# A decoder layer on one core: order of the prologue and of the first body changed on five queues

## What is computed

```python
x = x + self_attention(layernorm(x))          # 16 heads of 16, rotary positions, causal window of 64
x = x + cross_attention(layernorm(x), ctx)    # 16 heads of 8 over 256 channels, mask rows and columns
x = x + experts(layernorm(x))                 # 8 experts, top 2 by sigmoid score + bias, and a shared one
```

## Time and profile before

| | us |
|---|---|
| median of 3 runs (lowest, highest) | 422.46 (421.8, 425.17) |
| the profiled execution, own time | 422.43 |
| its span, first to last instruction | 420.6 |
| PE busy / DVE busy / ACT busy / POOL busy | 330.3 / 271.1 / 140.1 / 103.7 |
| mean granted clock of TensorE | 0.886 |

### The profile page before, as it was taken

One profiled execution on the slowest core, in us unless ns is written; L12 is line 12 of the kernel. 1 busy time (PEld: TensorE's weight loads), 2 busy tenths in 40 slices (PEclk: granted clock), 3 DMA queues, 4 the chain that ended last, 5 costly groups with the idle time before them and its releaser, 6 DMA issues.

```text
span 420.6 us, 6660 instructions
## 1 busy us (share of the span) xinstructions
PE 330.3 (79%) x2532; PEld 207.6 (49%) x2550; DVE 271.1 (64%) x500; ACT 140.1 (33%) x221; POOL 103.7 (25%) x125
## 2 busy tenths in 40 slices
PE   2685875694667979779979789998774979979787
PEld 2563443451322436458733336884222646636676
DVE  4557895299634387966872788778477445543755
...
DMA packets 31115, 28.27 MB, mean 67 GB/s; under 512 B 5964, under 2 KB 28204, under 8 KB 31084
## 3 DMA queue, kind: packets, MB, share of 16 engines
...
## 4 chain that ended last, share of the span: by engine, by line
PE 49%; DVE 22%; issue 10%; ACT 6%; SPq 5%; DMA 4%; POOL 3%; DVEq 0%; POOLq 0%; ACTq 0%
PE ps L941 13%; PE ps L975 6%; PE ps L863 5%; DVE max L1777 5%; PE ps L620 4%; ACT prob L1264 4%; PE ps L841 3%; PE ps L798 3%; SPq L440 2%; PE ps L631 2%; DVE max L1716 2%; DVE o1s L1731 2%; PE ps L884 1%; PE ps L659 1%; DVE u L1830 1%
## 5 line engine op out<-in xcount | busy, mean ns | idle before, releaser
L1777 DVE TENSOR_REDUCE max<-ps 128x4 f32<-128x1024 f32 x64 | 77.0, 1220 | 39.1 <-PE ps L798 39.1
L1264 ACT ACTIVATE prob<-ps 128x1024 f32<-128x1024 f32 x64 | 63.9, 1026 | 58.9 <-PE ps L841 58.7
L941 PE MATMUL ps<-xn1T,w_sb 128*128 128x256 f32 (+1 forms) x360 | 76.0, 360 | 6.1 <-DVE u L1830 5.6
L941 PEld LDWEIGHTS ps<-xn1T,w_sb 128*128 128x128 f32 x360 | 61.4, 201 | 17.1 <-DVE u L1830 7.5
L1508 POOL TENSOR_TENSOR u_times_u<-u 128x256 f32<-128x256 f32 (+1 forms) x45 | 29.1, 647 | 106.3 <-DVE u L1830 65.4
L863 PE MATMUL ps<-prob,v 128*32 128x256 f32 x512 | 41.9, 417 | 7.0 <-ACT prob L1264 6.7
L975 PE MATMUL ps<-w_sb,hT 128*128 128x256 f32 x144 | 40.5, 401 | 5.2 <-DVE hT L1839 5.2
L1716 DVE TENSOR_REDUCE max<-ps 128x4 f32<-128x512 f32 x32 | 21.3, 686 | 23.3 <-PE ps L659 23.2
L1244 ACT ACTIVATE prob<-ps 128x512 f32<-128x512 f32 x32 | 19.1, 598 | 45.6 <-PE ps L687 45.6
L1300 ACT ACTIVATE tanh_u<-u 128x256 f32<-128x256 f32 (+1 forms) x45 | 16.7, 372 | 49.7 <-DVE u L1830 45.2
L1830 DVE TENSOR_TENSOR u<-ps,g_bc 128x512 f32<-128x512 f32 (+1 forms) x40 | 23.2, 580 | 14.2 <-PE ps L941 9.6
...
## 6 DMA issues: line engine op xcount, KB each, us to landing
...
```

What stands on the lines that cost most here:

```text
L941: mm = pe.matmul(ps[:, banks_of(i, batches).up[n % 2], D * w + cols.start:D * w + cols.stop], w13_sb[:, e, k, w, :], xn3T[:, k, cols], sta ...
L1264: act.activation(prob[:, 2 * (u % 4):2 * (u % 4) + 2, :], ps[:, bank:bank + 2, :], ACT.Exp).then_inc(exp2, 1)
L1777: v.tensor_reduce(max2[:, a].rearrange("p t (j u) -> p j t u", j=2)[:, :, :, u], ps[:, bank:bank + 2, :].rearrange("p j (t s) -> p j t s", ...
```

## The change

In the prologue ScalarE copies pair 1's tokens between its casts of pair 0's query and key; TensorE does the key and value projections of cross pair 0 ahead of the turn of the maxima; the three memsets of the mask rows go to the start of VectorE's program and the five copies to ScalarE, behind `self_out(0, 1)`, with semaphores `mrow_fills` and `mrow_copies`. On SyncE the key's parts of pair 0 go before the store of the mask rows, `load_x(2)` goes before the mask rows' loads, the experts' first six weights are loaded in one piece behind the query's parts of pair 0, the key's parts of pair 1 go right behind `scores_b1` 16 and ahead of the maxima of batch 0, and the maxima of batch 1 go behind the first part of the query of pair 1. In body 0 `out` goes behind `exp 0` and `max 3`, `query` behind `max 5` and `exp 3`, `turn` ahead of `exp 6`, with residual, norm, bias and casts one or two groups later. The wait for the experts' weights counts four DMAs instead of six.

```diff
--- before.py
+++ after.py
@@ -104,11 +104,11 @@
 SPREAD = ((SEL, 1), (DOWN, 2))
 LAST_PAIR = (1, 1, 1, 2, 1, 2, 1, 2)
 FIRST_STEPS = ((), (), (0, 1), (2,), (3,), (4,), (5,), (6,), (7,))
-FIRST_JOBS = (("max", 0, 1, ("max", 8)), ("max", 1, 2, None), ("max", 2, 1, ("max", 9)), ("out", 0, 0, None),
-              ("exp", 0, 0, None), ("max", 3, 2, ("max", 10)), ("exp", 1, 1, ("max", 11)), ("max", 4, 2, ("max", 12)),
-              ("exp", 2, 0, ("exp", 1)), ("query", 0, 0, None), ("max", 5, 2, ("max", 13)), ("exp", 3, 1, ("exp", 2)),
+FIRST_JOBS = (("max", 0, 1, ("max", 8)), ("max", 1, 2, None), ("max", 2, 1, ("max", 9)), ("exp", 0, 0, None),
+              ("max", 3, 2, ("max", 10)), ("out", 0, 0, None), ("exp", 1, 1, ("max", 11)), ("max", 4, 2, ("max", 12)),
+              ("exp", 2, 0, ("exp", 1)), ("max", 5, 2, ("max", 13)), ("exp", 3, 1, ("exp", 2)), ("query", 0, 0, None),
               ("max", 6, 2, ("max", 14)), ("exp", 4, 0, ("exp", 3)), ("max", 7, 2, ("max", 15)),
-              ("exp", 5, 1, ("exp", 4)), ("exp", 6, 0, ("exp", 5)), ("turn", 0, 0, None), ("exp", 7, 1, ("exp", 6)))
+              ("exp", 5, 1, ("exp", 4)), ("turn", 0, 0, None), ("exp", 6, 0, ("exp", 5)), ("exp", 7, 1, ("exp", 6)))
 FIRST_BANKS = (2, 3, 0, 7)
 LEAD = ((0, 1), (2,), (3,), (), (4,), (5,), (6,), (), (7,))
 
@@ -296,7 +296,9 @@
         first_mid = [sem(f"first_{n}_mid") for n in "qk"]
         first_low = [sem(f"first_{n}_low") for n in "qk"]
         consts = sem("consts")
+        mrow_fills = sem("mrow_fills")
         mrow_chain = sem("mrow_chain")
+        mrow_copies = sem("mrow_copies")
         mrow_st = sem("mrow_st")
 
         var_ready = [sem(f"var_ready{n}") for n in range(3)]
@@ -491,7 +493,7 @@
                                  rows.broadcast_to([P, 2, cols.stop - cols.start])).then_inc(g_ld[q], 16)
 
             def mask_rows_store():
-                sp.wait_ge(mrow_chain, 11)
+                sp.wait_ge(mrow_copies, 5)
                 for n, rows in enumerate((mrow_q, mrow_k)):
                     for j in range(2):
                         sp.dma_start(d_mrow[n, :, :, j].rearrange("b s d t -> b s (d t)"),
@@ -552,32 +554,32 @@
             sp.wait_ge(v2_proj, 1)
             load_ctx(1)
             load_masks(1)
-            mask_rows_store()
             for c in range(3):
                 cross_part(0, 1, c)
-            load_experts(0, 3)
+            mask_rows_store()
+            sp.wait_ge(x1_ready, 1)
+            load_x(2)
             sp.wait_ge(mrow_st, 16 * 4)
             cross_mask_rows(0)
-            sp.wait_ge(x1_ready, 1)
-            load_x(2)
             for c in range(3):
                 cross_part(0, 0, c)
-            load_experts(3, 6)
+            load_experts(0, 6)
+            sp.wait_ge(scores_b1, 16)
+            for c in range(3):
+                cross_part(1, 1, c)
             cross_max(0, 0)
             for c in range(3):
                 self_part(2, c)
-            sp.wait_ge(scores_b1, 16)
             cross_mask_rows(1)
-            for c in range(3):
-                cross_part(1, 1, c)
             load_ctx(2)
             load_masks(2)
             sp.wait_ge(x1_ready, 2)
             load_x(3)
-            for c in range(3):
+            cross_part(1, 0, 0)
+            cross_max(0, 1)
+            for c in (1, 2):
                 cross_part(1, 0, c)
             load_experts(6, 9)
-            cross_max(0, 1)
             self_max(2)
             for i in range(1, PAIRS - 2):
                 body(i, True, True, True)
@@ -921,7 +923,7 @@
                 if n > 1:
                     pe.wait_ge(u_ready, u - 1)
                 if u == 0:
-                    pe.wait_ge(ld_experts, 16 * 6)
+                    pe.wait_ge(ld_experts, 16 * 4)
                 if n == 0:
                     pe.wait_ge(ez_ready, i + 1)
                     wait(pe, u_ready, 9 * i)
@@ -1075,9 +1077,9 @@
             pe.wait_ge(consts, 2)
             for c in range(8):
                 self_max_scores(0, c)
-            self_turn_max(0)
             cross_project_keys(0)
             cross_project_values(0)
+            self_turn_max(0)
             for step in range(9):
                 if step < 8:
                     self_exp_scores(0, step, (MISC, 0))
@@ -1373,9 +1375,9 @@
             act.dma_start(bqk_sb[:, 0:1], bq).then_inc(ld_cross, 16)
             act.dma_start(bqk_sb[:, 1:2], bk).then_inc(ld_cross, 16)
             act.dma_start(bv_sb[:], bv.broadcast_to([P, P])).then_inc(ld_cross, 16)
-            for n in range(2):
-                first_high_part(n)
+            first_high_part(0)
             self_tokens(1)
+            first_high_part(1)
             for n in range(2):
                 first_mid_part(n)
             act.wait_ge(first_high[1], 1)
@@ -1399,6 +1401,12 @@
                 if c == 4:
                     self_out(0, 0)
             self_out(0, 1)
+            act.wait_ge(mrow_chain, 10)
+            for r in (2, 3):
+                act.copy(mrow_q[:, 3 * r:3 * r + 3, :], mrow_q[:, 3:6, :]).then_inc(mrow_copies, 1)
+            for c in range(3):
+                src = mrow_q[:, c:c + 1, :]
+                act.copy(mrow_k[:, 3 + 3 * c:6 + 3 * c, :], src.broadcast_to([B, 3, D])).then_inc(mrow_copies, 1)
             cross_high(0, 0)
             cross_mid(0, 0)
             self_turn_max(1)
@@ -1421,9 +1429,9 @@
             for kind, u, pair, free in FIRST_JOBS:
                 if kind == "exp":
                     exponential(0, 0, u, pair)
-                    if u == 2:
+                    if u == 4:
                         cross_high(1, 0)
-                    if u == 4:
+                    if u == 6:
                         cross_mid(1, 0)
                 elif kind == "turn":
                     turn_max(0, 1)
@@ -1646,15 +1654,13 @@
                 ins.then_inc(ready, 1)
                 chain.end()
 
-            mrow = Chain(dve, mrow_chain, 11)
+            mrow = Chain(dve, mrow_chain, 10)
 
             def mask_rows():
 
                 mrow.start(0)
+                dve.wait_ge(mrow_fills, 1)
                 dve.wait_ge(mall_ld, 16)
-                v.memset(mrow_q[:, MASK_ROWS:2 * HD2, :], 0.0)
-                v.memset(mrow_k[:, MASK_ROWS:2 * HD2, :], 1.0)
-                v.memset(mrow_k[:, 0:3, :], 1.0)
                 mrow.link(v.tensor_scalar(m_pen[:], m_all[:], -1.0, 1.0, ALU.mult, ALU.add))
                 mrow.link(v.tensor_scalar(m_pen[:], m_pen[:], -NEG, None, ALU.mult))
                 for n, src in enumerate((m_pen, m_all)):
@@ -1666,14 +1672,7 @@
                         mrow.link(v.tensor_tensor(part[2], m_r[:, n, :], part[1], ALU.subtract))
                 v.tensor_tensor(mrow_q[:, 5, :], m_r[:, 1, :], mrow_q[:, 4, :], ALU.subtract).then_inc(mrow_chain, 1)
                 mrow.n += 1
-                dve.wait_ge(mrow_chain, mrow.n)
-                for r in (2, 3):
-                    v.tensor_copy(mrow_q[:, 3 * r:3 * r + 3, :], mrow_q[:, 3:6, :])
-                for c in range(3):
-                    src = mrow_q[:, c:c + 1, :]
-                    ins = v.tensor_copy(mrow_k[:, 3 + 3 * c:6 + 3 * c, :], src.broadcast_to([B, 3, D]))
                 assert mrow.n == 10
-                ins.then_inc(mrow_chain, 1)
 
             mp1 = Chain(dve, mp1_chain, 3)
             mp2 = Chain(dve, mp2_chain, 3)
@@ -1936,6 +1935,9 @@
                 cross_max_parts(i, 1)
                 second_batch(i, has_self, has_next)
 
+            v.memset(mrow_q[:, MASK_ROWS:2 * HD2, :], 0.0)
+            v.memset(mrow_k[:, MASK_ROWS:2 * HD2, :], 1.0)
+            v.memset(mrow_k[:, 0:3, :], 1.0).then_inc(mrow_fills, 1)
             dve.wait_ge(small_fills, 1)
             self_norm(0)
             dve.wait_ge(ld_ident, 16)
@@ -1988,10 +1990,10 @@
             for kind, u, pair, free in FIRST_JOBS:
                 if kind == "max":
                     cross_max(0, 1, u, pair)
-                    if u == 2:
+                    if u == 3:
                         self_residual(1)
                         cross_norm(1)
-                    if u == 4:
+                    if u == 5:
                         cross_query_bias(1)
             cross_max_parts(0, 1)
             second_batch(0, True, True)
```

## The result

The changed kernel took 407.84 us (median of 4 runs, 403.36 to 412.66), the kernel before 423.81 us in the same comparison (4 runs, 421.8 to 430.58): a ratio of 0.964, 95% interval 0.954 to 0.975. Executions of one kernel come in two states, and the ratio is taken from the fast ones, the medians from all. The forecast was 415.0, with 411.8 to 418.8 as its range. The direction was right; the gain was about twice the one forecast.

A forecast was written before the change was run, and what follows sets the result against it. The prediction took no single engine as the bound but chains of dependent steps and their waits, chiefly for pair 2's normalised tokens and `stack_1k<-parts`. Sum: 0 + 0 - 2.3 - 5.1 = -7.4, 422.43 to 415.0 us, range 411.8 to 418.8.

The forecast's parts named there:

- Prologue and mask rows: Start through the mask-row work: about 0 for the prologue, bounds -1.5 and +3, and 0 on the path for mask rows.
- early tokens: Prologue: token copy between the casts starts projections earlier; of 4 us on TensorE only 0.5 is left at the scores.
- both new gaps: Prologue: TensorE idle about 24 to 28 and 39 to 43 us, opened by the change.
- Load of x: Before 75.89 us: VectorE's 3.27 us wait for pair 2's x goes, token turn earlier; -2.3, bounds -2.4 and -1.2.
- second rival: Clock: slow work follows both new gaps, pair 0's exponent steps all take 1.5 us; +3, total 418.0; 12%.
- The stage behind it: After pair 2's token turn, up to 97.6 us: on-chip work only shifts along, no further gain.
- First body: ScalarE's 7.19 us wait for the key's transfers goes; batch 1 starts 7.4 earlier, 5.1 new, unknown ends -3 and -6.5.
- third rival: First body: shorter gap before max scores 5 keeps the clock up for query and values; another -1.5, 413.5; 15%.
- From the scores of batch 1 on: Everything behind batch 1's start, about 126 us: depends on these starts alone, shifts as a whole, no further gain.
- first rival: First body's stall is only replaced: body gives 2.5 instead of 5.1, x load 1.8, total 418.1; 15%.
- slow copies: Fourth rival, mask rows: ScalarE copies at 4.0 us each delay the load of x; +5, total 427.4; 4%.
- shift eaten later: Fifth rival: a later wait (key's transfers or pair 2's masks) eats the shift, no gain, 422; 9%.

The follow-up runs named there:

- b_lock: The kernel before, with GpSimd's low part of pair 1 waiting until the parts of the first maxima are written; ratio 0.994 of the kernel before (0.988 to 0.9997).
- u_keys: The changed kernel with the context's key and value projections behind the first turn of the maxima again; median 410.68 us (4 runs).
- u_x: The changed kernel with the load of x for pair 2 behind the mask rows' loads again; ten runs between 416.7 and 422.6 us.
- a_again: The changed kernel run once more, nothing edited; no total is stated, its batch 1 stage took 20.5 us against 22.0 in the first profile.
- a_lock: The changed kernel with GpSimd's low part of pair 1 waiting for the parts of the first maxima; median 409.25 us.
- u_row: The changed kernel with the row of batch 1's maxima behind all the query's parts and the load of experts again; 421.78 us, 0.9985 of the kernel before.
- u_jobs: The changed kernel with the old jobs table put back (order of output projection, query, turn, residual, norm, bias, casts); median 409.11 us.

## Why the forecast was off

**Prologue and mask rows, 0: right.** The 0.5 us of the early tokens did not appear at 28.82, the mask rows were hidden as said. The 0 holds for the sum of the stage and not for its parts: both new gaps are followed by slow work. The -2.0 in the profile is the draw against GpSimd: b_lock, the kernel before with none held, has 37.6 and 30.9, the kernel after 37.5 and 29.9. With the -0.5 of the next column it lies outside the bounds of -1.5 to +3 and has another reason than they named. Copies on ScalarE: forecast 0.8 each, measured 0.77.

**Load of x, -2.3: right, -2.6.** The row of pair 1's maxima was put at 3.7 us from issue to landing "as the row issued at 39.93 did"; that row was used at 44.03, 4.1 behind, which changes 74.1 to 74.5 and nothing in the sum. The second rival, slow work behind the two new gaps, came true in part: 0.63 us for the first scores at 28.82 (0.39 before) and for the exponent steps until 45.1, but not for all of them. It did not show as a loss of the two stages against the kernel before, which had its own slow steps until 48.4, and by ending later than the new ones they hid the cost of the second gap; u_keys, without the second gap, is about 2 us shorter there.

**The stage behind it, 0: wrong, -1.7 to -2.6.** "Everything up to 97.6 is on-chip and shifts along" took work for fixed that is done at either clock. The wait that was taken away had also kept the clock down: 0.50 until 82 us before, 1.00 from 72.8 in the changed kernel. With the wait put back (u_x) the stage is 25.9; without it 23.9, and 23.0 in a_again and a_lock.

**First body, -5.1: right, -5.8.** The steps followed one by one hold: max scores 5 were forecast at 112.6, the query at 114.6, the turn at 121.5, and they came at 107.64, 109.61 and 116.27, each 5.0 to 5.2 earlier, of which 4.6 had been gained before the body began. The first body was the part with the longest working and, in this profile, a small error. The query ran in 2.08 us, the slow level, so the third rival's saving did not come here; in a_again it did in part (1.82 us, scores at 0.39), behind a gap that was no shorter (2.69 us against 2.51), and the body was at 20.5, -7.3. The forecast gave one cause for the wait's end, the transfers; the runs showed two, either of which is nearly enough.

**From the scores of batch 1 on, 0: wrong, -2.9.** "The rest depends on these starts alone, so it shifts as a whole" is the step that failed, in the same way: the earlier trace rows showed a wait and 0.50 behind it, a few microseconds ahead of this stretch, and were used only as a threat to the change, never as something it could give back. Some of the 2.9 is the kernel before's own bad draw: b_lock has 19.5 in this stage, 0.6 less. The first rival (418.1), the slow copies (427.4) and the shift eaten later (422) are out.

**The row's place.** The forecast had it issued at 122.35 and the scores 4.0 behind it. It was issued at 116.99 and the scores ran 3.9 behind, without a wait for the row: TensorE's own leftovers ended then, as the forecast had also said. But all this stood inside one term. As a term of its own it would have shown what hangs on it: 7 us in the stages of u_row, and in its median the whole gain.

**Sum.** Without the draw and the last column the profile gives -0.5 - 2.6 - 1.7 - 5.8 - 2.9 = -13.5. The forecast's two terms are 8.4 of that, the two from the clock 4.6, and -0.5 is in pair 1's turn. The medians differ by 16.0, and 15.2 against the longer series of the kernel before; the 2 us left over are smaller than the spread of each kernel and stay open. So does why the medians of u_x and u_row are 13.5 and 13.9 us above the changed kernel where the stages they touch hold 6.4 and 7.0. The two together would be 27.4, more than there is to lose. No version that ran beats the changed kernel by more than that spread: u_jobs and a_lock were at 406.97 and 406.99 in the profile, 409.11 and 409.25 as medians.
